# Sorted expert tiles: operands turned in pairs, results kept in pairs, deeper rings

## The reference

```python
# layer 0, GELU experts, 128 -> 512 -> 128
for eid in range(e):
    w = jnp.sum(jnp.where(idx == eid, vals, jnp.zeros((), x.dtype)), axis=-1)
    h = jax.nn.gelu(x_flat @ w1[eid].T, approximate=False)
    y = h @ w2[eid].T
    out = out + w[:, None] * y
# layer 3, gated experts, 128 -> 1024 -> 512 -> 128
h = xf @ wa.T + ba
h1, h2 = jnp.split(h, 2, axis=-1)
h = jax.nn.silu(h1) * h2
return h @ wb.T + bb
```

## Time and profile before

| | us |
|---|---|
| median of three runs | 4925.69 |
| their lowest and highest | 4912.45, 4927.64 |
| the profiled execution | 4909.32 |
| its span, first to last instruction | 4907.4 |
| mean granted TensorE clock, share of full speed | 0.853 |

### The profile page before, as it was taken

The page is one execution under the profiler, slowest core; times in us unless marked ns, Lnnn a source line. Parts: engine busy times, 40 slices in busy tenths (PEclk is TensorE's granted clock), DMA queues, the critical chain, the costliest instruction groups (busy, mean ns, idle before and its releaser), DMA issues. The chain is left out here.

```text
span 4907.4 us, 71549 instructions
## 1 busy us (share of the span) xinstructions
PE 3529.0 (72%) x20958; PEld 2298.0 (47%) x20958; DVE 3231.1 (66%) x6387; ACT 2362.5 (48%) x4454; POOL 2120.6 (43%) x2029
## 2 busy tenths in 40 slices
PE   6867566768884548886448888749974878767686
PEld 4657355723332423333322222236653658745586
DVE  5430772069997267884349899977877766666665
ACT  3334433455651327774235455446753645544345
POOL 0046004649993435553227788721222116401254
PEclk9879777989997769997668898969986879979798
DMA  2011101145551223320223344300000001100012
GB/s 88 21 33 43 44 21 34 43 105 91 93 92 31 81 71 91 93 64 12 58 96 67 67 72 69 66 20 1 1 3 3 0 28 40 66 10 0 34 39 79
DMA packets 223543, 241.36 MB, mean 49 GB/s; under 512 B 38845, under 2 KB 170660, under 8 KB 221460
## 3 DMA queue, kind: packets, MB, share of 16 engines
q1 hardware_dynamic: 200980, 192.20, 17.0%
q0 software_dynamic: 22272, 45.66, 2.9%
HBM read 174.13 MB, written 62.72 MB: 48 GB/s over the span
## 5 line engine op out<-in xcount | busy, mean ns | idle before, releaser
L2452 PE MATMUL s_l_attn_a_y_ps<-XN,c_ident 128*128 128x512 f32 x1024 | 572.1, 670 | 94.6 <-POOL XN L2470 77.1
L2522 DVE TENSOR_TENSOR_SCAN s_l_attn_a_h<-s_l_attn_a_da,XN 128x512 f32<-128x512 f32 x512 | 608.2, 1210 | 22.3 <-POOL XN L2478 15.3
L2460 ACT ACTIVATE s_l_attn_a_da<-s_l_attn_a_delta,s_l_attn_a_a 128x510 f32<-128x510 f32 x512 | 346.0, 685 | 401.1 <-DVE s_l_attn_a_h L2522 398.0
L1086 POOL DMA_INDIRECT XNT<-rows_x,s_l_ffn_ffn_from_row x284 | 277.8, 978 | 464.4 <-DVE s_l_ffn_ffn_to_row L948 379.0
L960 DVE COPY s_l_ffn_ffn_xt<-s_l_ffn_ffn_turned 128x128 f32<-128x128 f32 x284 | 79.7, 291 | 555.9 <-PE s_l_ffn_ffn_turned L1161 244.3
L1091 POOL DMA_INDIRECT rows_y<-PICK,s_l_ffn_ffn_to_row x284 | 296.8, 1045 | 296.4 <-ACT PICK L1032 237.9
L1172 PE MATMUL s_l_ffn_ffn_up<-s_l_ffn_ffn_xt,s_l_ffn_ffn_own_w 128*128 128x128 f32 x2272 | 337.2, 296 | 103.6 <-DVE s_l_ffn_ffn_xt L960 100.7
L4390 DVE TENSOR_REDUCE s_l_attn_b_top<-s_l_attn_b_m_ps 128x2 f32<-128x512 f32 x512 | 330.2, 688 | 83.3 <-PE s_l_attn_b_m_ps L4096 79.4
L1182 PE MATMUL s_l_ffn_ffn_down<-down,s_l_ffn_ffn_hid 128*128 x2272 | 328.5, 291 | 75.6 <-DVE s_l_ffn_ffn_hid L974 47.7
L2452 PEld LDWEIGHTS s_l_attn_a_y_ps<-XN,c_ident 128*128 128x128 f32 x1024 | 185.0, 203 | 420.4 <-POOL XN L2470 292.2
L1172 PEld LDWEIGHTS s_l_ffn_ffn_up<-s_l_ffn_ffn_xt,s_l_ffn_ffn_own_w 128*128 128x128 f32 x2272 | 307.5, 210 | 114.6 <-DVE s_l_ffn_ffn_xt L960 111.6
(11 more groups left out here) (722 smaller groups left out, 8521.2 us busy)
## 6 DMA issues: line engine op xcount, KB each, us to landing
LOG<-s_l_attn_a_c_kept SPq DMA_DIRECT2D x128, 256.0 KB, 4.2
s_l_attn_a_more_c_rows<-s_l_attn_a_c_kept SPq DMA_DIRECT2D x128, 256.0 KB, 4.2
s_l_attn_a_b_rows<-s_l_attn_a_c_kept SPq DMA_DIRECT2D x192, 64.0 KB, 3.5
s_l_attn_b_qr<-s_l_attn_b_q_rows SPq DMA_DIRECT2D x64, 144.0 KB
s_l_attn_b_kr<-s_l_attn_b_k_rows SPq DMA_DIRECT2D x64, 144.0 KB
rows_x<-XN SPq DMA_DIRECT2D x8, 1024.0 KB, 3.9
XN<-rows_y SPq DMA_DIRECT2D x16, 512.0 KB, 5.1
XNT<-rows_y SPq DMA_DIRECT2D x16, 512.0 KB, 8.3
```

The source lines that it names most:

```text
L1086: nc.gpsimd.indirect_dma_start(xin[j % RING], None, k.rows_x[:, :], bass.IndirectOffsetOnAxis(from_row[:, j:j + 1], 0)).then_inc(gathered[ ...
L2452: last = self.nc.tensor.matmul(self.y_ps[:, i, :], self.k.ident[:], self.hc[n % 2][:, i, :], start=(n == 0 and not begun), stop=(n == NST ...
L2460: self.nc.scalar.activation(self.da_half(g, n, i)[:, :, 1:], self.delta[par][:, i, :].rearrange("p (b t) -> p b t", b=BPG)[:, :, 1:], ACT. ...
L2522: self.nc.vector.tensor_tensor_scan(self.h[n % 2][:, i, :], self.da_half(g, n, i).rearrange("p b t -> p (b t)"), self.u[n % 2][:, i, :], 0 ...
```

## The change

In `sorted_experts` alone, with one constant beside it:

- PE turns two tiles in a row into one PSUM bank, and one DVE copy of 256 columns takes both (`take_xt(n)` for the tiles 2n and 2n + 1); there are 36 copies where there were 71. The turning waits for both gathers and is done four to five tiles ahead of the step's index, not two.
- `down` of two tiles goes to the two halves of one bank, and one ACT copy of 256 columns (`keep_y(n)`) keeps both. `go_down` is run two tiles behind the index, not one.
- `xt`, `own_w1` and `hid` are rings of six (`xt` as three buffers of two tiles). An ungated stage has four `up` banks, a gated one still two.
- The rings of row buffers `xin` and `yout` have 14 tiles, not 12, and the scatter lies 12 tiles behind the gather.

The diff's core, with the lines that only follow from it left out:

```diff
-    RING, LAG = 12, 10
+    RING, LAG = ROWS_RING, ROWS_RING - 2
+    HELD, UPS = 6, 2 if gated else 4
+    LEAD, DOWN_LAG = 4, 2
+    DUOS = -(-NT // 2)
...
-        up = s.two_ps("up", [P, chunks, P])
+        up = [s.ps(f"up{i}", [P, chunks, P]) for i in range(UPS)]
...
+        def duo(n):
+            return min(2, NT - 2 * n)
...
+            def take_xt(n):
+                dve.wait_ge(turned_up, n + 1)
+                since(dve, up_ready, 2 * n - HELD + 2)
+                nc.vector.tensor_copy(xt2[n % 3][:, 0:duo(n) * P], turned_ps[n % 2][:, 0:duo(n) * P]).then_inc(xt_ready, 1)
...
             for j in range(NT):
-                if j + 2 < NT:
-                    take_xt(j + 2)
+                if j % 2 == 1 and j + LEAD - 1 < NT:
+                    take_xt((j + LEAD - 1) // 2)
...
+            def keep_y(n):
+                act.wait_ge(down_ready, 2 * n + duo(n))
+                for j in range(2 * n, 2 * n + duo(n)):
+                    if j >= RING:
+                        act.wait_ge(scattered[j % RING], 16 * (moved[j % RING] + j // RING))
+                nc.scalar.copy(yout2[n % (RING // 2)][:, 0:duo(n) * D], down[n % 2][:, 0:duo(n) * D]).then_inc(y_ready, 1)
...
             for j in range(NT):
-                if j + 2 < NT:
-                    take_w1(j + 2)
+                if j + LEAD < NT:
+                    take_w1(j + LEAD)
...
                     act.wait_ge(up_ready, j + 1)
-                    since(act, down_ready, j - 2)
-                    nc.scalar.activation(hid[j % 3][:], up[j % 2][:], ACT.Gelu).then_inc(hid_ready, 1)
-                if j > 1:
-                    keep_y(j - 2)
-            keep_y(NT - 2)
-            keep_y(NT - 1)
+                    since(act, down_ready, j - HELD + 1)
+                    nc.scalar.activation(hid[j % HELD][:], up[j % UPS][:], ACT.Gelu).then_inc(hid_ready, 1)
+                if j % 2 == 0 and j >= DOWN_LAG + 2:
+                    keep_y((j - DOWN_LAG - 2) // 2)
+            for n in range((NT - DOWN_LAG - 1) // 2, DUOS):
+                keep_y(n)
...
+            def turn(n):
+                since(pe, xt_ready, n - 1)
+                for i in range(duo(n)):
+                    j = 2 * n + i
+                    pe.wait_ge(gathered[j % RING], 16 * (moved[j % RING] + j // RING + 1))
+                    last = nc.tensor.transpose(turned_ps[n % 2][:, i * P:(i + 1) * P], xin[j % RING], k.ident[:])
+                last.then_inc(turned_up, 1)
...
-            for j in range(NT + 1):
-                if j + 2 < NT:
-                    turn(j + 2)
+            for j in range(NT + DOWN_LAG):
+                if j % 2 == 0 and j + LEAD < NT:
+                    turn((j + LEAD) // 2)
                 if j + 1 < NT:
                     go_up(j + 1)
-                if j > 0:
-                    go_down(j - 1)
+                if j >= DOWN_LAG:
+                    go_down(j - DOWN_LAG)
```

59 lines of the change are left out of this document (25 added, 34 removed).

## The result

| us | before | changed |
|---|---|---|
| median | 4920.12 (20 runs) | 4929.15 (20 runs) |
| lowest to highest | 4903.13 to 4934.45 | 4912.79 to 4952.27 |
| span of the profiled execution | 4907.4 | 4926.1 |
| mean granted TensorE clock | 0.853 | 0.844 |

The changed kernel takes 1.0026 of the time of the one before (95% interval 1.0015 to 1.0037), 13 us more by the ratio and 9 by the medians: slower, by an amount whose middle lies within the 0.3% that I called no change. I had forecast 4834, and the range ended at 4920: a miss of 95 us.

A forecast was written before the change was run, and what follows sets the result against it. POOL's issues and waits for late PE news were taken to bound ungated loops, PE gated ones; 2 x (29.5 - 4) + 2 x (24 - 4) = 91 us off 4925.7 gave 4834 us, range 4775 to 4920.

The forecast's parts named there:

- The bound: Ungated loops: POOL fullest at 2.56 us per tile plus 43.0 us of waits for late PE news; gated loops: PE fullest.
- The step that failed: Ungated stages: deeper rings let PE run three steps, 5.7 us, without news, covering the 4.8 us lag, so nearly all waits go.
- the quarter kept: Share of the removable waits assumed to remain: 10 us per ungated stage, 8 us per gated stage.
- The 29.5 us: Gain per ungated stage: 39.5 us of POOL's waits that can go, less 10 us kept.
- the sign that I named for them: Changed profile: the forecast is wrong if the lag grows with the rings, waits then being fewer and as long in total.
- The first: Rival: news is late until POOL pauses, lags stretch, a third of the waits gained; 32 us, 4894 us; chance 0.18.
- the second: Rival: pauses free the news and paired results lengthen each pause, so the kernel is slower, 4963 us; chance 0.10.
- TensorE is as slow as its news: Rival: PE's work itself is late and bounds ungated loops at 3.1 us per tile, rings give nothing; 4942 us; chance 0.08.
- Gated: Gated stages: 32.4 us of PE's waits at the down for `hid` can go, 8 kept, so 24 us gained per stage.
- Nothing is counted for their own time: The 35 DVE and 35 ACT copies saved per stage: no gain counted, at most 0.29 us each, 10 us per stage.
- a part of 4 us: The 4 us per stage taken for the opening, which includes the first result's wait for its pair.
- The opening: Start of each stage: two more gathers ahead of the first scatter cost 2.5 us, late news more; 4 us taken per stage.

The follow-up runs named there:

- e3: The changed kernel with second weights at a fixed address, so PE loads no register for the expert number; 4935.33 us, ratio 1.0026.
- e7: The kernel before with row rings of 14 and the scatter 12 tiles behind the gather, nothing else changed; 4895.21 us, ratio 1.0002.
- e15: The changed kernel without any pairs, with the scatter 9 tiles behind the gather, not 12; 4945.08 us, ratio 1.0051.
- e1: The changed kernel with all gathers and scatters of the four loops issued by SyncE as plain DMAs on consecutive rows; 4648.27 us, ratio 0.9445.
- e12: The changed kernel without its pairs: tiles turned and results kept one by one, everything else as changed; 4947.32 us, ratio 1.0065.
- e13: The changed kernel with results kept one by one, tiles still turned in pairs; 4899.44 us, ratio 0.9961.
- e14: The changed kernel with tiles turned one by one, results still kept in pairs; 5011.60 us, ratio 1.0204.
- e8: The kernel before (ring 12) with the first scatter behind the 7th gather, not the 11th; 4888.92 us, ratio 0.9986.
- e2: The changed kernel with only the scatters issued by SyncE as plain DMAs to consecutive rows, gathers still by POOL; 4729.19 us, ratio 0.9609.
- e5: The changed kernel with four memsets on POOL ahead of each scatter, each waited for, a break of 1.37 us a tile; 5055.27 us, ratio 1.0331.
- e4: The changed kernel with one 64-column memset on POOL ahead of each scatter, waited for, a break of 0.45 us; 4942.38 us, ratio 1.0047.
- e18: The kernel of e16 with DVE's copy of the turned pair moved behind `gate_hid` and `shift` of the same tile; 4730.49 us, ratio 1.0029.
- e6: The changed kernel with the scatter 8 tiles behind the gather, not 12, ring still 14; 5516.61 us, ratio 1.1270.
- e11: The kernel before (ring 12) with the first scatter behind the 6th gather; 4940.40 us, ratio 1.0095.
- e16: The changed kernel with results kept singly, and in ungated stages turnings two ahead, downs one behind, scatter distance 7; 4728.63 us, ratio 1.0031.

## Why the prediction was wrong

**The bound.** Right for the kernel before: POOL's issues and its waits make the ungated loop, and what waits for PE's work starts late. The two kernels and the ten variants of them that issue everything from POOL without added breaks and have room (e3, e7 to e15) ran with late news, and all have first ungated loops of 215 to 224 us, whatever the lead, pairs, ring or distance. One small misreading of the earlier trace rows: the 1.95 us after the last gather's end are those of ACT's GELU (291.94); the copy at 292.06 comes 2.07 after.

**The step that failed** is "In an ungated stage PE can now go on without any news for three steps more, 3 x 1.89 = 5.7 us, against the lag of 4.8 in the steady part", and with it the quarter kept. Two things in it were wrong. The lag is no constant: in the first ungated loop nine copies in ten were within 4.8 us before, 6.4 after, and DVE's longest idle stretch went from 6.9 to 10.7. POOL issued eight DMAs in a row, not six, and the pause grew with it, from 1.8 to 2.2 to 2.8, so that a pause costs 0.30 us an issue before (1.8 / 6) and 0.31 changed (2.5 / 8). And PE doesn't go on at 1.89 us a step in that time, and that is where the freed time went: it crawls, 35.6 us of "issue" gaps and 9.7 us of busier matmuls where 50.1 us of waits for `xt` are gone. The 29.5 us that the sum took as gained per ungated stage were nothing: 43.0 us of POOL's waits became 45.3.

**The rivals.** The first two had part of it right, pauses that grow with the runs between them, and the changed profile shows the sign that I named for them: waits "fewer and as long in total". The first was priced at a third of the waits gained, the second said that it decides "from the point at which POOL's pauses don't become rarer". They did become rarer, 23 to 17, and so much longer that the sum stayed (43.0 and 45.3 us). "TensorE is as slow as its news" had 0.08 and the nearest of the rivals' times (4942 for a measured 4929), and in the changed kernel its mechanism is the one that shows: PE fills the loop and waits for others for 9.9 us of 222.3. I held against it that news came several at once. That stands for the earlier trace rows, where two tiles turned 1.9 us apart are copied together. The changed round doesn't show it: the result that ACT copies at 400.37 is that of the down of 392.07, which had ended at 393.13, just ahead of the turning that DVE copies at 400.41, so both are 7.1 to 7.2 us late and in PE's order. Whether PE's work was late there or only its news, the trace can't say. The Trainium skill says in "Perfetto Trace Analysis", section Tensor Engine Instruction (MATMUL, LD_WEIGHTS), that a matmul's end is computed and not observed. That fits here: the busy time of 174.35 us for matmuls that take 137.33 in e1 can't be told apart from gaps inside the records.

**Gated.** I had 24 us gained per stage from the waits of PE's down. The first loop went from 257.1 to 261.5, the second from 258.2 to 257.2. The same step failed: the waits went, 38.9 us of them, and PE's gaps and busier matmuls took 37.9 back. By e12, e13 and e14 the parts are: rings, lead and distance +12 to +16 us (e12's 267.5 against 255.6 and e7's 251.9, on other chips), where I had 24 gained; pairs of turnings -31 (236.4 against 267.5) or -37 (the changed kernel's 259.8 against e14's 296.6), where I had counted nothing; pairs of results +29 or +23, where I had counted a part of 4 us. I wrote "Nothing is counted for their own time", and looked at the copies' 0.29 us, not at what stands behind a copy in DVE's queue. The row was there: the copy at 4182.07 ahead of the `hid` of 4182.28, a cost that I put down to `hid` alone.

**The opening.** Forecast 4 us later per stage; it is 5.2 in the ungated ones (22.4 against 17.2) and 7 in the first gated one. Right in kind; but e7 and e8 say that 2 to 8 us of opening hardly reach the end of an ungated loop, perhaps because POOL's number of issues is the same.

**What was shown and what wasn't.** Shown: late news and slow TensorE come with DMAs that POOL issues (e1, e2), a break of 1.4 us every two issues frees them and one of 0.45 doesn't (e5, e4, on two chips), deeper rings took PE's waits away and PE's slower work took their place (the two profiles), the ring alone does nothing (e7), paired turnings gain and paired results cost in the gated stages (e12 to e14). Argued from waits alone: that the paired turning gains because DVE's queue is no longer blocked; e18 was to test that, and met a chip on which nothing is late. Open: what holds the news and slows PE; whether it is POOL's issuing or the indirect kind of DMA, which no run separates; why POOL's waits add up to 41 to 49 us in each of the twelve first ungated loops; and why the number of issues between two pauses is six or eight.

## What to carry to other kernels

Where an engine's news comes late while another engine is busy issuing, don't price deeper rings by the engine's undisturbed cadence: here the engine that no longer had to wait worked slower instead, the issuer ran longer between its waits, and their sum stayed. Take the issuing away first, or try it, before deepening the rings. Count for each result how many inputs beyond its own must have been fetched before it can leave; lead, distance and pairs use up that room, and the ring must pay for it. Pair an operation where a late wait blocks other work in the same queue, and don't pair the one whose second half somebody waits for.

## What the hardware showed that I had not expected

- While POOL issues indirect DMAs back to back (one per 1.28 us), DVE's copies start up to 8 us and more after the recorded end of PE's work in steady rows (8.0 in e4, 8.9 in e12) and 15.5 us in a burst of 14 gathers (e2), and PE's own stream has gaps of up to 1.1 us between matmuls that have their operands (changed kernel). With the same bytes moved by SyncE's plain DMAs the copies start 0.04 us after it by the median, and the kernel takes 5.6% less time than before (e1).
- It isn't there on every chip: on one of the four chips of e1 to e18 131 issues in a row held nothing, and the kernel before ran in 4716.54 us there, 3.6 to 4.1% under its 4894 to 4920 on the others.
- The mean granted TensorE clock in the ungated loops, where 1.0 is the 2.4 GHz level, was 0.78 (e6) to 0.95 (e11) in the kernels in which PE starves or crawls, and 0.98 in e1 and e16 to e18, where it doesn't.
